# Attention slots with weighing in two pieces, earlier transposes of x, and a first slot without lag

## The reference

```python
x = x + 0.5 * ffn(layernorm(x))
x = x + attention(layernorm(x))
x = x + 0.5 * ffn(layernorm(x))

def attention(x):                      # 16 heads of 8
    q, k, v = proj(Wq, bq), proj(Wk, bk), proj(Wv, bv)
    a = softmax(q @ k.T * 8 ** -0.5)
    return (a @ v) @ Wo.T + bo

def ffn(x):                            # 128 -> 512 -> 512 -> 512 -> 128, ternary weights
    h = silu(x @ w1.T * s1) * (x @ w2.T * s2)
    h = gelu(h @ h1.T * t1)
    h = gelu(h @ h2.T * t2)
    return h @ w3.T * s3
```

## Time and profile before

| what | us |
|---|---|
| median of 3 runs (lowest, highest) | 619.1 (618.34, 622.76) |
| the profiled execution | 617.05 |
| its span | 615.2 |
| PE busy | 589.1 (96%) |
| ACT busy | 466.4 (76%) |
| DVE busy | 443.6 (72%) |
| POOL busy | 98.3 (16%) |
| slots 0 to 15, from PE's first maximum scores of slot 0 to its first work behind slot 15 | 204.17 to 430.36 |

### The profile page before, as it was taken

One profiled execution on the slowest core, in us unless ns is written; L12 is line 12 of the kernel. 1 busy time (PEld: TensorE's weight loads), 2 busy tenths in 40 slices (PEclk: granted clock), 3 DMA queues, 4 the chain that ended last, 5 costly groups with the idle time before them and its releaser, 6 DMA issues.

```text
span 615.2 us, 12580 instructions
## 1 busy us (share of the span) xinstructions
PE 589.1 (96%) x4452; PEld 439.3 (71%) x4452; DVE 443.6 (72%) x1000; ACT 466.4 (76%) x796; POOL 98.3 (16%) x262
## 2 busy tenths in 40 slices
PE   2999999999999999999999999999989999999996
PEld 2788788788686766565656565766678878788785
DVE  7995855868558778798988897885665756855742
ACT  4677977968865578788787878877877977968964
POOL 2092020022021103132231302102020020020000
PEclk9999999999999799999999999999999999999999
DMA  8300000000074306171625343400000001000011
GB/s 282 86 2 1 0 2 1 0 0 1 1 273 145 130 2 220 56 255 62 235 89 187 137 139 142 134 2 1 2 1 1 1 1 36 0 26 8 1 34 37
DMA packets 36693, 42.02 MB, mean 68 GB/s; under 512 B 2464, under 2 KB 27296, under 8 KB 36640
## 3 DMA queue, kind: packets, MB, share of 16 engines
q1 hardware_dynamic: 36640, 41.31, 19.8%
HBM read 22.42 MB, written 18.87 MB: 67 GB/s over the span
## 4 chain that ended last, share of the span: by engine, by line
PE 73%; ACT 9%; DVE 8%; issue 5%; DMA 3%; SPq 1%; POOL 0%; ACTq 0%; DVEq 0%; POOLq 0%
PE bank L1092 39%; PE bank L1204 9%; PE bank L1179 8%; PE bank L1191 4%; PE bank L1193 3%; DVE silu L842 3%; DVE act_lo L833 2%; ACT silu L544 2%; DVE neg_max L883 2%; PE bank L1161 1%; PE bank L1222 1%; PE bank L1169 1%; ACT act_hi L536 1%; ACT act_hi L559 1%; DMA QK<-qk_scratch 1%
## 5 line engine op out<-in xcount | busy, mean ns | idle before, releaser
L1092 PE MATMUL bank<-act_hi,WH 128*128 128x512 f32 x576 | 230.5, 400 | 3.8 <-ACT act_hi L559 1.5
L1092 PE MATMUL bank<-act_lo,WH 128*128 128x512 f32 x576 | 225.7, 392 | 0.0
L883 DVE TENSOR_REDUCE neg_max<-bank 128x2 f32<-128x512 f32 x256 | 166.8, 681 | 32.6 <-PE bank L1179 30.4
L678 ACT ACTIVATE probs<-bank 128x512 f32<-128x512 f32 x256 | 139.3, 598 | 38.6 <-PE bank L1193 37.0
L853 DVE TENSOR_TENSOR act_lo<-full,act_hi 128x512 fp32r<-128x512 f32 x128 | 91.5, 719 | 101.7 <-ACT act_hi L559 101.4
L557 ACT ACTIVATE full<-bank,SG 128x512 f32<-128x512 f32 x128 | 88.1, 688 | 65.8 <-PE bank L1092 65.0
L1092 PEld LDWEIGHTS bank<-act_hi,WH 128*128 128x128 f32 x576 | 108.2, 188 | 31.2 <-ACT act_hi L559 4.7
L1092 PEld LDWEIGHTS bank<-act_lo,WH 128*128 128x128 f32 x576 | 108.3, 188 | 23.1 <-issue 1.0
L1191 PE MATMUL bank<-QK 32*128 32x256 f32 x512 | 96.1, 334 | 0.4 <-ACT probs L678 0.4
L559 ACT ACTIVATE act_hi<-bank,SG 128x512 fp32r<-128x512 f32 x128 | 87.1, 681 | 0.0
L1193 PE MATMUL bank<-m_parts,SEL 32*128 32x256 f32 x512 | 82.1, 280 | 0.0
(11 more groups left out here) (94 smaller groups left out, 570.7 us busy)
## 6 DMA issues: line engine op xcount, KB each, us to landing
qk_scratch<-qk SPq DMA_DIRECT2D x64, 256.0 KB, 2.6
QK<-qk_scratch SPq DMA_DIRECT2D x16, 1024.0 KB, 7.6
raw_rest<-w_ffn SPq DMA_DIRECT2D x4, 512.0 KB, 5.8
out<-X SPq DMA_DIRECT2D x4, 512.0 KB, 3.2
X<-x SPq DMA_DIRECT2D x3, 512.0 KB, 7.7
raw<-w_ffn SPq DMA_DIRECT2D x3, 256.0 KB, 4.5
X<-x SPq DMA_DIRECT2D x2, 256.0 KB, 3.2
WA<-w_att SPq DMA_DIRECT2D x1, 256.0 KB, 5.6
```

The costliest lines, as they stand in the source:

```text
L678: A.activation(probs[:, v % 8, :], bank[B_BANKS[bb][v]][:, :], ACT.Exp, scale=SCALE)\
L883: D.tensor_reduce(neg_max[:, bb, qt, n0:n0 + 2], bank[(banks or A_BANKS[bb])[u]][:, :].rearrange("p (h k) -> p h k", h=2), axis=AX.X, op=A ...
L1092: ins = MM(dst, a, b, start=k == 0, stop=k == len(todo) - 1)
```

## The change

The weighing of some groups is cut in two: kt = 0 is issued at v = 5, 9, 13 or 17, two steps before kt = 1. Which groups these are is in `EARLY_HALF`: steps 1 and 9 of an even slot and 1 and 5 of an odd one; in slots 0 and 1 all of them. Bank 6 gets another order. Even slot: tokens at step 9 (before 13), V at 11 (before 9), the transposes of x at 13 (before in the odd slot at 7). Odd slot: q at 7 and k at 9 (before 9 and 11), tokens at 13 as before. V waits for `o_norm` of the batch whose tokens stand at step 9, x for `v_set`, q for `att_added`, the tokens of the even slot for `att_added`. On DVE the four normalisings of x move to steps 7, 8, 9 and 12, behind the scaling. Slot 0 has no lag: v = u, V of pair 1 at step 1 and x of pair 2 at step 3; the split of its maxima stands between the two residuals, and the wait for the second residual stands at v = 2. Slot 1 has only the last weighing of batch 0 in its first steps.

```diff
-TOKENS = 13
+TOKENS = (9, 13)
+EARLY_HALF = ((1, 9), (1, 5))
...
-        def in_step(u, prev, own=True):
-            at = [(0, u - SKEW)] if own else []
+        def in_step(u, prev, own=True, second=False):
+            at = [(0, u - SKEW if prev else u)] if own else []
             if prev:
-                at.append((1, u - SKEW + UNITS))
+                at.append((1, u + UNITS if second else u - SKEW + UNITS))
...
@@ scalar, attend @@
+                if not prev:
+                    top_max(b, 4)
...
-                    if u == (9 if prev else 5) and v_pair is not None:
+                    if u == (11 if prev else 1) and v_pair is not None:
                         set_v(*v_pair)
-                    if u == 7 and ahead is not None:
+                    if u == (13 if prev else 3) and bb == 0 and ahead is not None:
                         x_to_sbuf(ahead)
-                    if u in (9, 11) and ahead is not None:
-                        full_part(ahead, (u - 9) // 2)
-                    if u in (10, 12) and ahead is not None:
-                        high_part(ahead, (u - 10) // 2)
+                    if u in (7, 9) and bb == 1 and ahead is not None:
+                        full_part(ahead, (u - 7) // 2)
+                    if u in (8, 10) and bb == 1 and ahead is not None:
+                        high_part(ahead, (u - 8) // 2)
...
@@ vector, end of the feed-forward half @@
                         residual(nb + 2 * i, 8 * i, 0)
+                        if into_att:
+                            split_max(0, 0, 4)
                         residual(nb + 2 * i + 1, 8 * i + 4, 1)
...
@@ vector, attend @@
-                    if u == (2 if prev else 0):
-                        split_max(b, bb, 6 if prev else 4)
+                    if u == 2 and prev:
+                        split_max(b, bb)
...
-                    if u == TOKENS + 1 and prev:
+                    if u == TOKENS[bb] + 1 and prev:
                         norm_o(b - 1)
-                    if u == TOKENS + 2 and prev:
+                    if u == TOKENS[bb] + 2 and prev:
                         scale_o(b - 1)
...
                     even = {u: lambda t=t: normalise(n, tile0 + t, t, 1, last=t == 3)
-                            for t, u in enumerate((8, 9, 10, 11))}
+                            for t, u in enumerate((7, 8, 9, 12))}
...
-                    odd = dict(zip((4, 5, 7, 8, 9, 11), norm_steps(norm_of(q), 4 * q, 4, halves=True)))
+                    odd = dict(zip((4, 7, 8, 9, 10, 11), norm_steps(norm_of(q), 4 * q, 4, halves=True)))
...
@@ tensor, attend @@
                 def rows_of_max():
-                    if prev2:
+                    if bb == 1 and pair + 2 < NPAIR:
+                        pe.wait_ge(a_xT_sb, pair + 3)
+                    elif bb == 1 and pair + 1 < NPAIR:
+                        pe.wait_ge(v_set, pair + 2)
+                    else:
                         pe.wait_ge(o_norm, b - 1)
-                    elif prev:
-                        pe.wait_ge(v_set, pair + 2)
                     max_rows(b, bb)
...
+                early = EARLY_HALF[bb] if prev2 else (1, 5, 9, 13)
...
-                            if not prev:
-                                pe.wait_ge(x_added, NB + CREDIT)
+                        if d == 0 and v == 2 and not prev:
+                            pe.wait_ge(x_added, NB + CREDIT)
...
+                        if v >= 5 and v % 4 == 1 and u in early:
+                            weigh(*at, v // 4 - 1, 0)
                         if v >= 7 and v % 4 == 3:
-                            weigh(*at, v // 4 - 1, 0)
+                            if u - 2 not in early:
+                                weigh(*at, v // 4 - 1, 0)
                             weigh(*at, v // 4 - 1, 1)
...
-                    if u == (9 if prev else 5) and v_pair is not None:
+                    if u == 7 and bb == 1 and ahead is not None:
                         if prev2:
                             pe.wait_ge(att_added, b - 1)
                         pe.wait_ge(m_lo, b + 1)
+                        project_q(ahead, 6)
+                    if u == 9 and bb == 1 and ahead is not None:
+                        pe.wait_ge(q_full, ahead)
+                        project_k(ahead, 6)
+                    if u == TOKENS[bb] and own and prev:
+                        if bb == 1 and ahead is not None:
+                            pe.wait_ge(k_full, ahead)
+                        else:
+                            pe.wait_ge(att_added, b - 1)
+                        tokens_of_o(b - 1)
+                    if u == (11 if prev else 1) and v_pair is not None:
+                        if prev:
+                            pe.wait_ge(o_norm, b)
+                        else:
+                            pe.wait_ge(x_added, NB - 1 + CREDIT)
                         project_v(v_pair, 6)
-                    if u == 7 and ahead is not None:
-                        if prev2:
-                            pe.wait_ge(att_added, b - 1)
-                        pe.wait_ge(m_lo, b + 1)
+                    if u == (13 if prev else 3) and bb == 0 and ahead is not None:
                         pe.wait_ge(v_set, pair + 2)
                         transpose_att(ahead, 0, 6)
```

More of the change, by code:

```diff
@@ L694, in attend @@
             def attend(b, bb, prev=True, prev2=True, own=True, steps=UNITS, ahead=None, v_pair=None):
+                second = prev and own and not prev2
+                if not prev:
+                    top_max(b, 4)
                 for u in range(steps):
-                    for d, v in in_step(u, prev, own):
+                    for d, v in in_step(u, prev, own, second):
                         if v < UNITS:
```

26 lines of the change are left out of this document (8 added, 18 removed).

## The result

The changed kernel took 641.56 us in the median of five runs (638.34 to 646.39), the kernel before 619.1 in five runs beside it (615.51 to 622.76): ratio 1.036, 95% interval [1.028, 1.043]. It is slower, as forecast, but by 21 us where 12 were reckoned, and the median lies 0.6 us outside the range. The profiled execution took 638.34 us.

A forecast was written before the change was run, and what follows sets the result against it. It took the attention stage as a chain on PE with small gaps. Steady slots +12.2, late +3.6, start -3.9 gave +11.9 on 617.05, so 629.0; the median lying 2 higher, it predicted 631 us, range 618 to 641.

The forecast's parts named there:

- The steady part: Slots 2 to 11: even slots 13.36 to 16.15 us, odd 15.44 to 15.07; +2.4 per pair of slots, +12.2 in all.
- V 2.42 after its pair: Even slots: V needs bank 6 and so scaling L904, 2.36 + 0.09 after the pair's start; PE stands 1.2 us.
- x 0.9: Even slots, step 13: the transposes of x wait 0.9 us for the last normalising, behind the maximum of step 12.
- slots 12 to 15: Late slots: slot 12 +2.3 us by the V wait, 13 and 14 +0.6 and +0.8, 15 -0.1; together +3.6.
- A half weighing: Each slot's split weighings on PE: a half estimated at 0.57 us, at least 0.50, at most 0.69; a whole cost 1.00.
- PE's work sets the pace: Rival, attention slots: DVE's results always ready, halves at 0.50, pair of slots 27.3 us, total 606; chance 0.10.
- the waits are hidden: Rival, steady slots: halves cost as reckoned but V and x do not wait; about 620 us, no change; chance 0.10.
- Slot 0: First slot: pairs of 0.9 us within 0.69 to 0.95, clock stays 1.00; 12.7 us against 15.62, -2.9.
- its start of -3.9 us: Slots 0 and 1 together: -2.9 and -1.0 us, giving -3.9.
- Slot 1: Second slot: loses four transposed units, a weighing and the x transposes; 13.4 us against 14.46, -1.0 (bounds 0 to -2).
- The sentence on the thin steps 0 to 3: Rival: clock falls at the entry or in slot 1's thin start, gain of 2.9 gone, 634 us; chance 0.07.
- Clock in the steady slots: Rival: idle waits of 1.2 and 0.9 us make the clock fall; two to five falls give 637 to 646; chance 0.13.

The follow-up runs named there:

- Four experiments: Kernel before with only the new bank 6 order (643.7 us) or half weighings (626.35); changed kernel with earlier even-slot scaling L909 (641.29) or last normalising at step 10 (637.45).
- the strips apart: Changed kernel with batch 1's maximum scores reordered (u xor 4), so a step's two units in slot 0 use different 32 rows: 640.11 us, ratio 1.035.
- the waits filled: Changed kernel with the strips apart, plus unused full matmuls in slot 1 and ahead of V and x in even slots: 634.25 us, ratio 1.022.
- DVE's steps early: Changed kernel with the strips apart and odd slots' small normalisation steps at 4, 5, 6, 7, 8, 11, ahead of POOL's work: 648.61 us.
- each filled kernel: Unused full matmuls added to before's slot 0 (614.71 us), the start-only kernel's slot 1 (615.47), the changed kernel's waits (634.25), or the changed kernel with all mends (629.03).
- the last normalising early: Changed kernel with the last of the even slot's four normalising steps moved from DVE's step 12 to step 10: 637.45 us, ratio 1.028.

## Why the prediction was right in part

- **The steady part: right.** 16.20 and 15.03 against 16.15 and 15.07, though the sum took slot 11 of before as 15.44 where it is 15.03, so nothing is gained there; V 2.42 after its pair (2.45 forecast), 1.2 idle, x 0.9, both released as named; slots 12 to 15 +3.5 (+3.6). A half weighing was 0.57 (277.84 + 0.69 = 278.53, V could have started at 279.10). Four experiments isolated or took away one term each (order, halves, scaling, normalising), and the slots changed by it. Of the 2.43 to a pair of slots 1.76 are the order's and 0.67 the halves'. The rivals in which PE's work sets the pace or the waits are hidden fell with it.
- **Slot 0: the pair was mis-sized.** Here the prediction's sum failed first: its start of -3.9 us measured +1.1, by this term and the next. It saw that both units of a step use the same 32 rows and set a pair at 0.9 within 0.69 to 0.95, from six matmuls in 0.73 at the program's entry. It measured 1.26, outside the bounds, and 0.69 with the strips apart. The six of the earlier trace rows belong to three units on two strips, beside each other; here the two units of a step take one strip in turn, 0.35 for each, and whatever comes next in order waits as well, so a bound from a row with other strips was none. Eight pairs at 0.36 more are 2.9; slot 0 took 15.07, not 12.7 (+2.4 us).
- **Slot 1: the rival came beside the forecast.** Forecast 13.4; 14.06 without a fall, 16.13 with it (+2.7, of which 0.7 is the mis-sized slot and 2.1 the clock). The sentence on the thin steps 0 to 3 stood there as a rival with 0.07 and excluded the other half: slot 0's clock stayed up, as the forecast said, and slot 1's did not.
- **Clock in the steady slots: under-weighed.** It had 0.13. The argument against it, that V's full-width work was missing in the earlier trace rows, doesn't hold: the clock fell behind V. The profiled execution has one such fall (+1.5 us). The median run stands 3.2 above it, at a mean clock of 0.988 against 0.991; it was not profiled. With the waits filled (and the start mended) the kernel runs at 634. The rule of the Trainium skill quoted there (TensorE: Matmul & The Clock Gate, A second HAM failure mode: psum-queue depth-cycling) agrees in part: one steady even slot out of four fell in this profile, four out of four with DVE's steps early, none with the strips apart. As cases are not exclusive, their chances should have been read as what adds to the sum.
- **Not foreseen.** The hold of DVE (0.8 us in slot 3, in other kernels of this study up to four slots), and 1.3 us of start-up that varies by run. The account, in us: 11.9 forecast, + 2.4 slot 0, + 2.7 slot 1, + 1.5 clock in slot 6, + 0.8 the hold, + 0.5 rest of slots 2 to 15, + 1.3 start-up, + 0.2 behind slot 15: 21.3, against 21.2 in the spans.

What stays open: which executions lose the clock. Runs of one kernel differ by up to 18 us (DVE's steps early), the slower ones at lower mean clocks. The runs of each filled kernel lie within 4 us, but so do the four with the last normalising early, unfilled (2.6), so few runs do not settle it.

## What to carry to other kernels

When several engines share one PSUM bank by a hand-written order, a job belongs where the bank's last reader is already done: count from the producer's start through every instruction queued on the reader's engine, and put at least as much other work between. Price idle time of PE twice, once as time and once as a risk to its clock; where a wait can't go, matmuls without use that end inside it can keep the clock: they cost nothing in the even slots (16.20 with and without), but 1.3 us in slot 1. And read the rows (strips) of neighbouring matmuls before pricing them as parallel.

## What the runs showed of the hardware

- The granted clock falls to its lower level (1.2 of 2.4 GHz) not only after plain idleness: 5.0 us of slot 1 with narrow scores, two half weighings and short waits, printed as 4.89 busy, came ahead of 6.8 us at 0.50. Five added matmuls of 0.3 to 0.4 us each in before's slot 0 saved 3.6 us there and 6 in the median.
- Two units of scores on the same 32 rows run one behind the other, 0.35 us each, and hold back units on other rows queued behind them: 1.26 instead of 0.69 us for a pair of steps.
- A small DVE operation that starts beside a running POOL operation over 128x512 can last as long as it: 1.29 instead of 0.16 us. With the strips apart, in slot 7, it was not held:

```profile
322.36 1.34 POOL L472 TENSOR_TENSOR qk<-qk_full,qk 128x512 fp32r<-128x512 f32 x1 [2.23 <-ACT qk L577]
...
322.40 0.16 DVE L789 TENSOR_SCALAR var<-moments 128x4 f32<-128x4 f32 x1
```

The start here is 0.04 behind POOL's, in slot 3 of the changed kernel 0.11 (263.32, 263.43). The printed start does not decide it: with the strips apart DVE was held in slot 5 at 0.03 and in slot 9 at 0.04, and with the last normalising early it was not held in slot 3 at 0.11. The Trainium skill (SBUF — State Buffer, SBUF: two separate sides) says that POOL and a DVE instruction in a mode with two ports (or with two inputs in SBUF) share a pair of ports as an exclusive lock, which whoever starts first keeps for the whole instruction. The held case agrees. In the case above POOL is printed as first and DVE was not held; there POOL's instruction took 1.34, against 1.29 in slot 5 of the same kernel, as if it had waited. Which mode L789 runs in, and what decides, no run shows.
